# A decoder layer on one core: how the cross attention gets its softmax denominators, and where its score matmuls stand in the step

## The reference, cut to what matters

```python
q = (query @ Wq.T + bq)...; k = (key @ Wk.T + bk)...; v = (value @ Wv.T + bv)...
scores = jnp.einsum('bhtd,bhsd->bhts', q, k) * scale
scores = scores + attn_mask[None, None, :, :]
scores = jnp.where(pad, -jnp.inf, scores)
scores = scores + spatial_bias + directional_bias      # both are fside here
probs = jax.nn.softmax(scores, axis=-1)
out = jnp.einsum('bhts,bhsd->bhtd', probs, v)
return out.transpose(0, 2, 1, 3).reshape(B, T, E) @ Wo.T + bo
```

## Time and profile before

| what | value |
|---|---|
| median of 3 runs | 647.23 us |
| the profiled execution | 644.72 us, of which the span of its instructions is 643.0 us |
| granted TensorE clock over the span | 0.939 of full |
| PE / DVE / ACT / POOL busy | 530.4 / 498.3 / 428.8 / 383.9 us |
| first and last score group of a batch (PE L902) | 214.3 us, 473.7 us |

### The profile page before, as it was taken

How to read it: one execution, slowest core, us unless ns; L and a number is a source line. 1 busy time by engine, 2 the same in 40 slices (tenths; PEclk the granted TensorE clock), 3 DMA queues, 4 the chain that set the end, 5 groups by cost and what they waited for, 6 DMA issues and landing times. The chain is left out here.

```text
span 643.0 us, 16021 instructions
## 1 busy us (share of the span) xinstructions
PE 530.4 (82%) x4272; PEld 412.8 (64%) x4272; DVE 498.3 (78%) x1993; ACT 428.8 (67%) x1545; POOL 383.9 (60%) x431
## 2 busy tenths in 40 slices
PE   3888999999998668877778778787866899999986
PEld 3677877877876545555555555555544677788864
DVE  3667768768765746998999998989986688888872
ACT  3577677777673266999999999999995133233321
POOL 6236765564685466788888888888841244444430
PEclk9889999999997967998998998989997599999999
DMA  6900000000001633688787777777700000000000
GB/s 165 232 6 1 1 1 1 0 0 0 2 2 33 107 70 75 122 144 144 137 144 143 138 140 139 139 139 139 136 2 1 1 17 17 17 16 16 18 18 16
DMA packets 84422, 42.37 MB, mean 66 GB/s; under 512 B 4378, under 2 KB 84132, under 8 KB 84388
## 3 DMA queue, kind: packets, MB, share of 16 engines
q1 hardware_dynamic: 83234, 41.63, 34.2%
q10 hardware_dynamic: 1154, 0.33, 0.2%
HBM read 39.86 MB, written 2.10 MB: 65 GB/s over the span
## 5 line engine op out<-in xcount | busy, mean ns | idle before, releaser
L990 ACT ACTIVATE c_P<-c_P,c_min 128x128 f32<-128x128 f32 x512 | 200.4, 416 | 0.0
L887 POOL TENSOR_TENSOR c_bias<-c_fside,c_cm 128x2048 f32<-128x2048 f32 x32 | 145.5, 4546 | 7.5 <-DVE c_cm L881 7.5
L1051 DVE CUSTOM_DVE_ANT_0 c_P<-banks,c_bias 128x128 f32<-128x128 f32 x512 | 117.1, 285 | 14.5 <-PE banks L902 10.1
L990 ACT ACTIVATION_READ_ACCUMULATOR c_P<-c_P,c_min 128x1 f32 x512 | 110.1, 215 | 0.0
L946 PE MATMUL banks<-ident,c_P 128*128 128x128 f32 x512 | 82.5, 294 | 5.7 <-ACT c_P L990 3.8
L946 PEld LDWEIGHTS banks<-ident,c_P 128*128 128x128 f32 x512 | 61.3, 150 | 17.6 <-ACT c_P L990 10.1
L1080 DVE COPY shared<-banks 128x512 f32<-128x512 f32 x96 | 65.9, 686 | 6.1 <-PE banks L946 6.1
L1495 POOL TENSOR_TENSOR xs<-shared,xs 128x512 fp32r<-128x512 f32 x8 | 10.6, 1331 | 89.4 <-ACT xs L1327 89.4
L1260 PE MATMUL banks<-um,lb_s 128*128 128x512 f32 x192 | 57.5, 416 | 2.7 <-ACT shared L1317 1.9
L933 PE MATMUL banks<-x_wT,shared 128*128 128x128 f32 x64 | 15.5, 326 | 41.9 <-DVE shared L1075 41.9
L1317 ACT ACTIVATE shared<-banks,bi_col 128x512 f32<-128x512 f32 x32 | 22.0, 687 | 41.5 <-PE banks L1260 41.5
(11 more groups left out here) (197 smaller groups left out, 1437.0 us busy)
## 6 DMA issues: line engine op xcount, KB each, us to landing
c_fside<-in_fside_Bx16xSxS_dram SPq DMA_DIRECT2D x64, 512.0 KB, 7.1
c_ctx<-in_ctx_dram SPq DMA_DIRECT2D x32, 64.0 KB, 5.1
out_dram<-shared SPq DMA_DIRECT2D x8, 256.0 KB, 2.3
X<-in_x_dram SPq DMA_DIRECT2D x3, 512.0 KB, 5.3
kmask_sb<-in_mask_BxS_bf_dram SPq DMA_DIRECT2D x1, 512.0 KB, 7.1
X<-in_x_dram SPq DMA_DIRECT2D x2, 128.0 KB, 3.5
c_P<-in_L_ffn_wi_dram SPq DMA_DIRECT2D x1, 256.0 KB
c_P<-in_L_ffn_lora_B_dram SPq DMA_DIRECT2D x1, 256.0 KB
```

The costliest lines, as they stand in the source:

```text
L887: nc.gpsimd.tensor_tensor(fm[:, q, :, :], fs[:, q, :, :], bc(cm[:], XH), ALU.add).then_inc(C["fm"], 1)
L990: last = nc.scalar.activation(P[:, par, h, :], P[:, par, h, :], ACT.Exp, bias=mn[:, par, h:h + 1], scale=-1.0, accum_out=rsx[:, par, h:h + 1])
L1051: last = nc.vector.tensor_tensor_reduce(out=P[:, o, h, :], in0=score_bank(n + 1, i)[:, 128 * j:128 * j + 128], in1=fm[:, o, h, :], scale=- ...
```

## The change

- **Denominators.** The exponentials lose accum_out. A constant head_ones (padded like the values, 1.0 where a head's 8 columns are) is multiplied with the same turned weights: mix_values issues 16 more matmuls with 32 columns, into columns 128 to 255 of bank 7. ACT takes their logarithm (denominator_logs) and the exponential of its negative (denominators_inverted); DVE multiplies the outputs by that. The reciprocal, its spreading, its transpose and its copy are gone.
- **Scores.** all_scores becomes score(i), each with its own wait for the bank's last reader; groups 0 and 1 stand near the step's start, 2 and 3 near its end with the output projection between them. DVE reads them in the order 0, 1, 2, 3 as before, with other work between.
- **Biases.** Halves of 8 heads each, one batch ahead instead of two, with two mask buffers; the transfers are halves of heads too (128 rows x 8 heads) with a semaphore for each.
- **Moves.** The copy of the values goes from DVE to ACT; ACT's two copies of the turned inputs become one of 256 columns; inputs_turned comes first on PE and ACT.

The diff, cut to its core:

```diff
--- before.py
+++ after.py
-            fill(pool, (ones, 1.0), (twos, 2.0), (vp, 0.0), (in_head, 1.0), (before, 1.0))
+            fill(pool, (ones, 1.0), (twos, 2.0), (vp, 0.0), (head_ones, 0.0), (in_head, 1.0), (before, 1.0))
             keep(pool, before, ALU.is_gt, 0, [[1, E], [-1, E]], 0)
+            pool_step(pool, nc.gpsimd.memset(head_ones[:].rearrange("p (j w) -> p j w", j=XG)[:, :, 0:XD], 1.0))
...
-        cm = sb("c_cm", [128, 128])
+        cm = sb("c_cm", [128, 2, 128])
-        cT = sb("c_cT", [128, 2, 128])
+        xcT = sb("c_xcT", [128, 2, 2, 128])
...
         vp = sb("c_vpad", [128, 2, NI * VPAD])
+        head_ones = sb("c_ones", [128, VPAD])
         mn = sb("c_min", [128, 2, XH])
-        rsx = sb("c_sum", [128, 2, XH])
-        rc = sb("c_recip", [128, XH])
...
@@ -875,65 +875,62 @@
 
             return bank((FIRST_BANKS if first_batches(n) else SCORE_BANKS)[i])
 
-        def x_masks(dve, k):
-            need(dve, C["fm"], k)
+        def x_masks(dve, k, q):
+
+            need(dve, C["fm"], 2 * k - 2)
             km = kmask_sb[:, bass.ds(k * T, T)]
-            nc.vector.scalar_tensor_tensor(cm[:], km, -3.0e38, half_mask[:], ALU.mult, ALU.add).then_inc(C["cm"], 1)
-
-        def x_biases(pool, k, m, q):
+            nc.vector.scalar_tensor_tensor(cm[:, q, :], km, -3.0e38, half_mask[:], ALU.mult, ALU.add).then_inc(C["cm"], 1)
+
+        def x_biases(pool, k, m, q, half):
+
+            heads = slice(HALF * half, HALF * half + HALF)
             need(pool, C["cm"], k + 1)
-            need(pool, s_fs[q], 32 * (m + 1))
-            need(pool, C["tt"], 4 * k - 4)
-            nc.gpsimd.tensor_tensor(fm[:, q, :, :], fs[:, q, :, :], bc(cm[:], XH), ALU.add).then_inc(C["fm"], 1)
+            need(pool, s_fs[q][half], 16 * (m + 1))
+            need(pool, C["tt"], 4 * k - 6 + 2 * half)
+            nc.gpsimd.tensor_tensor(fm[:, q, heads, :], fs[:, q, heads, :], bc(cm[:, q, :], HALF), ALU.add).then_inc(C["fm"], 1)
 
 
-            def all_scores():
+            def score(i):
 
                 need(pe, C["q"], n + 2)
                 need(pe, C["kbd"], n + 2)
-                need(pe, C["tt"], 4 * n + 4)
+                if isinstance(n, int) and n < 2:
+                    need(pe, C["tt"], 4 * n + 4)
+                else:
+                    need(pe, C["tt"], 4 * n + i + 1)
                 if first_batches(n + 1):
                     need(pe, C["v"], n + 1)
-                for i in range(NI):
-                    rows = slice(32 * i, 32 * i + 32)
-                    nc.tensor.matmul(score_bank(n + 1, i), qx[rows, o, :], kbd[rows, o, :, :].rearrange("p j s -> p (j s)"),
-                                     start=True, stop=True).then_inc(C["sc"], 1)
+                    if project and i == 0:
+                        need(pe, C["T"], n + 3)
+                rows = slice(32 * i, 32 * i + 32)
+                nc.tensor.matmul(score_bank(n + 1, i), qx[rows, o, :], kbd[rows, o, :, :].rearrange("p j s -> p (j s)"),
+                                 start=True, stop=True).then_inc(C["sc"], 1)
 
...
-            def reciprocals_turned():
-                need(pe, C["rx"], n)
-                need(pe, C["oT"], n - 1)
-                nc.tensor.transpose(bank(7)[:, 0:128], rx[:].rearrange("p h d -> p (h d)"), ident[:]).then_inc(C["Rp"], 1)
-
...
@@ -950,32 +947,44 @@
 
                 need(pe, C["ptD"], 3 * n)
                 need(pe, C["ptA"], n)
-                need(pe, C["RT"], n)
                 need(pe, C["v"], n)
-                for j in range(XG):
-                    for i in range(NI):
-                        last = nc.tensor.matmul(bank(7)[32 * i:32 * i + 32, 0:128],
-                                                vp[:, o, VPAD * i + 32 * j:VPAD * i + 32 * j + 32],
-                                                PTs[:, o, i, 128 * j:128 * j + 128], start=(j == 0), stop=(j == XG - 1))
+                need(pe, C["oT"], n - 1)
+                for w in range(2):
+                    for j in range(XG):
+                        for i in range(NI):
+                            block = vp[:, o, VPAD * i + 32 * j:VPAD * i + 32 * j + 32] if w == 0 else head_ones[:, 32 * j:32 * j + 32]
+                            last = nc.tensor.matmul(bank(7)[32 * i:32 * i + 32, 128 * w:128 * w + 128], block,
+                                                    PTs[:, o, i, 128 * j:128 * j + 128], start=(j == 0), stop=(j == XG - 1))
                 last.then_inc(C["pv"], 1)
 
-            if scores:
-                all_scores()
+            def project_out():
+                need(pe, C["oT"], n)
+                need(pe, C["x2"], n - 1)
+                need(pe, C["v"], n + 2 if scores else min(n + 1, B))
+                nc.tensor.matmul(bank(0)[:, 0:128], oTs[:], x_wT[:, 3, :], start=True, stop=True).then_inc(C["yp"], 1)
+
             if project:
                 inputs_turned()
-            if finish:
-                reciprocals_turned()
+            if scores:
+                score(0)
+                score(1)
             if attend:
                 weights_turned(0)
-                weights_turned(1)
             if project:
                 queries_keys()
             if finish:
                 mix_values()
+            if scores:
+                values()
             if attend:
+                weights_turned(1)
                 weights_turned(2)
-            if scores or finish:
-                outputs_values()
+            if scores:
+                score(2)
+            if finish:
+                project_out()
+            if scores:
+                score(3)
             if attend:
                 weights_turned(3)
 
...
@@ -987,44 +996,61 @@
 
                 need(act, C["tt"], 4 * batch + i + 1)
                 for h in range(XG * i, XG * i + XG):
-                    last = nc.scalar.activation(P[:, par, h, :], P[:, par, h, :], ACT.Exp, bias=mn[:, par, h:h + 1], scale=-1.0,
-                                                accum_out=rsx[:, par, h:h + 1])
+                    last = nc.scalar.activation(P[:, par, h, :], P[:, par, h, :], ACT.Exp, bias=mn[:, par, h:h + 1], scale=-1.0)
                 last.then_inc(C["ex"], 1)
 
             def inputs_turned():
                 need(act, C["Tp"], n + 3)
-                need(act, C["yv"], n + 1)
-                nc.scalar.copy(xT2[:], bank(0)[:, 0:128])
-                nc.scalar.copy(cT[:, q, :], bank(0)[:, 128:256]).then_inc(C["T"], 1)
-
...
+            def values():
+                need(act, C["vp"], n + 2)
+                need(act, C["pv"], n)
+                dst = vp[:, o, :].rearrange("p (i j w) -> p i j w", i=NI, j=XG)[:, :, :, 0:XD]
+                nc.scalar.copy(dst, bank(0)[:, 128:256].rearrange("p (i j d) -> p i j d", i=NI, j=XG)).then_inc(C["v"], 1)
+
+            def denominator_logs():
+                need(act, C["pv"], n)
+                need(act, C["rc"], n - 1)
+                nc.scalar.activation(log_den[:], bank(7)[:, 128:256], ACT.Ln).then_inc(C["ln"], 1)
+
+            def denominators_inverted():
+                need(act, C["ln"], n)
                 need(act, C["oT"], n - 1)
-                nc.scalar.copy(RT[:], bank(7)[:, 0:128]).then_inc(C["RT"], 1)
+                nc.scalar.activation(inv_den[:], log_den[:], ACT.Exp, scale=-1.0).then_inc(C["rc"], 1)
...
+            if project:
+                inputs_turned()
             if attend:
                 exps(n, q, 1)
             if project:
-                inputs_turned()
-            if finish:
-                reciprocals_turned()
+                queries()
+                keys()
             if attend:
                 exps(n, q, 2)
-            if project:
-                queries_keys()
+            if finish:
+                denominator_logs()
+            if scores:
+                values()
+            if finish:
+                denominators_inverted()
             if attend:
                 exps(n, q, 3)
             if scores:
...
-            if project and not (isinstance(n, int) and n < 0):
-                x_masks(dve, n + 2)
+            if attend:
+                weights_turned(0)
             if norm:
                 statistics()
-                aggregates()
             if scores:
                 score(0)
-            if attend:
-                weights_turned(0)
+            if norm:
+                aggregates()
+            if project and not (isinstance(n, int) and n < 0):
+                x_masks(dve, n + 2, q)
             if scores:
                 score(1)
+            if finish:
+                outputs()
             if attend:
                 weights_turned(1)
-            if scores:
-                score(2)
+            if norm:
+                normalise()
             if finish:
-                outputs()
-            if scores:
-                score(3)
+                add_to_stream()
             if attend:
                 weights_turned(2)
             if scores:
-                values()
```

(23 more changed lines are left out.)

83 lines of the change are left out of this document (36 added, 47 removed).

## The result

The kernel after takes 706.05 us, median of 4 runs (704.32 to 709.33), against 645.95 us for the kernel before on the same chip (642.06 to 647.66). The ratio is 1.095, 95% interval 1.088 to 1.101. The forecast was 659 us and its range ended at 674: slower, as forecast, but by 60 us and not by 14. The profiled execution has a span of 702.5 us against 643.0, so 59.5 us more.

A forecast was written before the change was run, and what follows sets the result against it. PE was to become the bound at 8.25 us a step plus 0.1 of waits, 8.35 against 7.855: 27 steps +13.4, first steps +2, end -1, so +14.4 on 644.7 gives 659 us; range 641 to 674.

The forecast's parts named there:

- PE becomes the bound: Cross attention loop: PE's packed step of 8.25 us exceeds the old 7.855 and every other engine.
- the 0.86 of the earlier trace: Lower price in us for a lone score, from a 512-column matmul on all rows; 1.07 was taken instead.
- The entries into tiles: PE's step: coming from whole-array work into row or column tiles costs about 0.1 us each time.
- the 0.1 that I took off as counted twice: PE's step at the mixing: one handover of 0.1 us removed, 8.34 to 8.25 us.
- the allowance of 0.1 for waits: PE's step: 0.1 us kept of the old 0.7 us of short waits, making 8.35 us.
- All three engines would allow a step of 6.6 to 7.0 us: Loop: by their busy times ACT, DVE and POOL would allow this step, a gain of 0.9 to 1.2 us.
- PE hardly waits: Loop: going round the new step, other engines seldom hold PE; 0.1 us of waits kept.
- The clock rival: Loop: PE without its hole loses the full clock, step 9.2 us, +36 us, 681 us; chance 0.09 above 672.
- ScalarE: ACT's busy time per loop step falls from 7.7 to about 5.8 us, exponentials without sums costing 0.25 each.
- Prologue: First four steps with scores, ahead of the steady loop: +2 us, with -6 and +9 as ends.
- The 9.7 us of ScalarE's waits: First four score steps: ACT's waits for turned inputs, now standing first; 6 us come back at the favourable end.
- Tail: End behind the loop: shorter exponentials against ones, late logarithm and inversion: about -1 us, from -3 to +1.

The follow-up runs named there:

- a_all_rows: Kernel after with score groups 2 and 3 multiplied over all 128 rows instead of their 32: 671.45 us, ratio 1.046.
- pairs_apart: Kernel after with scores 2 and 3 together, projected output in its own bank, normalisation moved earlier and GpSimd's output_bias waiting for it: 646.36 us, ratio 1.007.
- a_wait: Kernel after with one wait changed: GpSimd's output_bias waits for the normalised input of the same step: 680.84 us, ratio 1.059.
- b_ones: Kernel before with the 16 matmuls with blocks of ones added behind the mixing, result unused: 638.51 us, ratio 0.992.
- a_own_bank: Kernel after with the projected output in columns of bank 7 instead of bank 0: 699.85 us, ratio 1.091.
- a_start: Kernel after with the old order for steps n below 2, four scores in a row at the head: 695.51 us, ratio 1.083.
- pairs_start: pairs_apart with the old order for steps n below 2, four scores in a row at the head: 640.71 us, ratio 0.995.
- a_pairs: Kernel after with score groups 2 and 3 issued together ahead of the output projection: 700.05 us (2 runs).
- pairs_ends: pairs_start with the old order also in the last steps (n of 28 and more): 644.85 us, ratio 1.003.
- a_together: Kernel after with all four score groups in a row behind queries and keys from step 2 on: 719.45 us, ratio 1.119.

## Why the prediction was right or wrong

**PE becomes the bound: right; the size of its step: short by 0.24 us.** Each part can be read off the step above. The lone scores cost 1.05 (I took 1.17 with the entry), so the choice against the 0.86 of the earlier trace rows was right, and a_all_rows shows that 0.86 holds only for all rows. The entries into tiles, which I had charged at 0.1 each, are there: queries and keys take 0.54 and the eight transposes 0.97 instead of 0.44 and 0.88. What I missed is the way out, which has a price too: the values behind the ones 0.32 instead of 0.22, the projection between two scores 0.42 instead of 0.22 (0.32 in pairs_apart, where it only has the way out), the transposes behind scores 0.49 instead of 0.44. Mixing and ones with their entry take 1.99 instead of 1.87, so the 0.1 that I took off as counted twice was there. 27 x (8.59 - 7.858) = +19.8 us instead of +13.4; the allowance of 0.1 for waits was not needed, since without the lock PE waits for nothing. Had this been the only error of the loop, the time would have been near 665, inside the range.

**"All three engines would allow a step of 6.6 to 7.0 us", and "PE hardly waits": this is the step that failed.** The busy times were right for these two (VectorE 182.04 / 27 = 6.7 and GpSimd 6.7 us in a_wait); the error is that they were summed engine by engine as if they were independent. The normalisation was moved to the middle of VectorE's step, and `output_bias` no longer kept GpSimd's additions behind it. I costed the first at nothing and the second at "6.6 stays". Measured: the step of 9.472 instead of 8.680 to 8.713, 21 us of the loop, and 25 us of the median for one wait (a_wait). Inside the loop of the kernel after, the steps above 8.59 sum to 255.7 - 27 x 8.59 = 23.8 us. The 21 ordinary steps carry 7.3 of it (on average 0.35 each: PE's wait for VectorE in one step, and in the next one a first pair of scores that lasts 1.26 us instead of 1.06), and the six low-clock steps, which sum to 68.0, the other 16.5.

**The clock rival** had the right sign and was put at 0.09. Its premise, that a PE without a hole loses the clock, does not hold: a_wait has PE at 100% and a clock of 0.99, and b_ones 1.00 against 0.96 between the same cuts of the kernel before. But how full PE is does not decide it either: a_own_bank has PE at 99.7% and a clock of 0.93. So the rule of the Trainium skill (TensorE: Matmul & The Clock Gate, "The HAM clock gate") that the prediction set against this rival, by which a fuller PE keeps the full clock, agrees with a_wait and b_ones and did not foretell the kernel after. Nor is it the length of PE's waits: the kernel after has 2.6 us of them behind the addition in its loop and 34.2 us of low clock, a_own_bank none and 34.1, a_all_rows 11.9 and 6.8. What stands together in the traces is the held normalisation (all five low-clock steps that have a step of the loop ahead of them follow one, but not every held one is followed by a low clock) with scores on 32 rows in the forms of the kernel after; what exactly decides it stays open.

**ScalarE** was forecast at 5.8 us a step and takes 187.57 / 27 = 6.9, because the exponentials without sums start 0.29 us apart (eight in 2.43 us, the last with its full 0.39), not 0.25. It had room, so this cost nothing. One table load and no accumulator reads: right.

**Prologue: +9.1, at the upper end of -6 to +9.** PE's busy time from 195 us to the first cut rose from 45.0 to 55.4 us and its idle time fell from 15.1 to 13.8: the loss is work at the low clock, not waits. The three steps with scores ahead of the cut have two passages of scores, or three, instead of one, and those at the low clock take 2.1 us each:

```profile
240.10 1.92 PE L943 MATMUL banks<-ident,c_P 128*128 128x128 f32 x8
241.95 2.08 PE L909 MATMUL banks<-shared,c_q 32*128 32x512 f32 x4
243.96 1.11 PE L943 MATMUL banks<-ident,c_P 128*128 128x128 f32 x4
...
249.40 2.08 PE L909 MATMUL banks<-shared,c_q 32*128 32x512 f32 x4
```

The 9.7 us of ScalarE's waits that I hoped for the earlier trace rows came back in part (L1005 waits 2.6 us), but they were not on the path. With the old order the first cut comes 3.5 us (a_start) to 8.3 us (pairs_start against pairs_apart) earlier, in executions that also differ in their clock, so the split between order and clock is not shown.

**Tail: +6.8 instead of -1.** About 3.3 of it is the first step behind the cut, again low-clock after a held normalisation: the tail is 182.6, and 179.3 in a_wait. The other 3.5 stay in nearly every form with scores 2 and 3 in the new place on 32 rows (178.1 to 179.3; 177.0 in pairs_start, 182.3 in a_pairs). In a_wait the last exponential ends 30.6 us behind the cut, 21.0 in the kernel before; my reading is that with nothing to overlap the late scores stretch the last steps. I had counted only instructions there, not the order. The one attempt to mend it, pairs_ends, did not separate this cleanly, so it is argued, not shown.

Together: PE's work +19.8, lock and clock in the loop +23.8 (a_wait, without the lock, gets 20.5 of them back), prologue +9.1, tail +6.8, which is the 59.5 us of the two spans.

## What to carry to other kernels

Before an order is changed, list for every moved instruction of VectorE that reads and writes SBUF what GpSimd runs at its new time; a wait of GpSimd that looks like a loss (24.5 us of idle before L1138 in the kernel before) may be what keeps the two apart, and giving it back is one line. Sum PE's step with a charge for the way into row or column tiles and one for the way out, and keep tiled work of one kind together. When PE binds, a small wait can cost more than itself: of the 14 waits of 0.17 to 0.3 us ahead of a step in the kernel after, six were followed by a step at the low clock, 1.8 to 3.5 us longer in the loop. No run here lets one foretell which, so measure the form without the wait. Work that lies in a hole of PE need not cost anything (b_ones).

## What the runs showed of the hardware

- A 128x128 float32 `tensor_scalar` from SBUF to SBUF on VectorE takes 0.34 us alone and up to 2.47 us beside GpSimd's addition of 2.35 us, ending 0.08 us behind it. Where it started 0.03 us ahead of the addition it was held to the addition's end, where it started 0.20 us ahead it was not. The mask, a `scalar_tensor_tensor` with two inputs in SBUF, takes 0.26 us alone and up to 0.74 us (pairs_start) when the end of an addition falls into it. Copies from PSUM (0.68 us) and the fused score instruction (0.28 us) kept their durations in the same stretches.
- A float32 product of 32 rows and 512 columns occupies PE for 1.05 us alone, two of them on two row groups 1.06 together, four on four 1.07 (kernel before), one on all 128 rows 0.86.
- 32 more records on PE in every step did not slow the kernel before, but gave 0.992 [0.989, 0.995], at a clock of 1.00 instead of 0.96 in the loop.
- Removing work from PE can slow a kernel: a_together has less work for PE than the kernel after and takes 13 us more; its normalisation meets GpSimd's addition in nearly every step.
- Regular steps can hold a low clock for long: a_together repeats 10.09 and 10.39 us at a granted clock of about 0.83 in its loop, a_pairs 9.06 and 11.1 to 11.5 for half of its loop.
- The clock of the loop depends on more than how busy PE is: low for 34.1 us with PE at 99.7% (a_own_bank), 7.0 us with PE at 100% (a_wait), 6.8 us with PE at 94% (a_all_rows).
